# Graph attention and a top-2 mixture of experts on one Trainium2 core: negated scores, routing moved four steps behind its group, and gates applied by GpSimd as it scatters

## What is computed

```python
x = x + gnn(layernorm(x), adj)       # x: 2048 x 128, adj: 2048 x 2048 of 0 and 1
x = x + ffn(layernorm(x))            # 64 experts, top 2 of them for each row

def gnn(n, adj):
    h = n @ W.T + b_W
    e = (h @ a1)[:, None] + (h @ a2)[None, :] + b_a
    e = where(e > 0, e, 0.2 * e)
    return softmax(where(adj > 0, e, -9e15), axis=1) @ h

def ffn(n):
    top, idx = top_k(n @ Wr + br, 2)
    gates = softmax(top)                                 # two gates for each row
    combine[row, idx] = gates                            # 2048 x 64
    return sum over e of combine[:, e] * (relu(n @ W1[e] + b1[e]) @ W2[e] + b2[e])
```

## Time and profile before

| | |
|---|---|
| median of 3 runs | 335.87 us (334.42 to 335.96) |
| the profiled execution | 333.78 us, span 332.0 us |
| busy over the span | PE 223.2 us, DVE 216.4, ACT 143.9, POOL 185.0 |
| attention loop on DVE, to the last leaky | 24.8 to 139.7 us |
| last attend ends, first gather starts | 151.3 and 178.4 us |
| experts at speed | 224 to 312.8 us |
| end stage | 312.8 to 332 us |

### The profile page before, as it was taken

The page is one execution under the profiler, slowest core; times in us unless marked ns, Lnnn a source line. Parts: engine busy times, 40 slices in busy tenths (PEclk is TensorE's granted clock), DMA queues, the critical chain, the costliest instruction groups (busy, mean ns, idle before and its releaser), DMA issues.

```text
span 332.0 us, 6227 instructions
## 1 busy us (share of the span) xinstructions
PE 223.2 (67%) x1797; PEld 212.2 (64%) x1797; DVE 216.4 (65%) x583; ACT 143.9 (43%) x313; POOL 185.0 (56%) x210
## 2 busy tenths in 40 slices
PE   0790888999589579793431510209999999999830
PEld 0760788989589478793320410209999989999830
DVE  3859999999999299756734000005666756676476
ACT  1146858888862477632500200015664333444400
POOL 5510068998779867887774777773234323333300
PEclk9997899999989859998555585558999999999995
DMA  6993505998976200010111632213555656664184
GB/s 162 158 183 66 102 0 94 287 248 217 238 197 190 105 17 2 24 34 25 48 48 37 180 88 64 56 40 105 162 155 160 179 147 172 170 178 136 34 243 137
DMA packets 29056, 40.55 MB, mean 122 GB/s; under 512 B 3744, under 2 KB 24416, under 8 KB 28000
## 3 DMA queue, kind: packets, MB, share of 16 engines
q1 hardware_dynamic: 23280, 25.14, 25.7%
q0 software_dynamic: 5376, 14.72, 20.0%
q10 hardware_dynamic: 368, 0.30, 0.5%
HBM read 43.27 MB, written 5.26 MB: 146 GB/s over the span
## 4 chain that ended last, share of the span: by engine, by line
PE 35%; DVE 20%; issue 18%; POOL 14%; DMA 4%; ACT 4%; another core or an unknown queue 4%; SPq 1%; DVEq 0%; POOLq 0%; ACTq 0%
PE bank L907 13%; PE bank L917 13%; POOL table L361 7%; DVE arena L570 6%; DVE xs L753 2%; POOL ve L341 2%; POOL rstd L343 2%; PE bank L785 2%; DMA xs<-in_x 2%; DMA arena<-result 1%; POOL rk L369 1%; PE bank L897 1%; PE bank L822 1%; PE bank L775 1%
## 5 line engine op out<-in xcount | busy, mean ns | idle before, releaser
L907 PE MATMUL bank<-arena 128*128 x380 | 61.4, 287 | 30.3 <-issue 19.8
L907 PEld LDWEIGHTS bank<-arena 128*128 128x128 f32 x380 | 52.2, 200 | 31.7 <-issue 31.5
L407 POOL DMA_INDIRECT result<-arena x32 | 30.8, 963 | 60.8 <-DVE arena L731 55.9
L487 ACT ACTIVATE arena<-bank,arena 128x128 f32<-128x128 f32 x95 | 34.9, 368 | 60.9 <-PE bank L907 31.5
L822 PE MATMUL bank<-arena 128*128 128x130 f32 x512 | 61.3, 278 | 0.0
L822 PEld LDWEIGHTS bank<-arena 128*128 128x128 f32 x512 | 59.9, 194 | 0.0
L917 PE MATMUL bank<-w2s,arena 128*128 x380 | 59.1, 279 | 1.0 <-issue 1.0
L731 DVE SCALAR_TENSOR_TENSOR arena<-bank,arena 128x128 f32 x95 | 33.3, 351 | 39.6 <-PE bank L917 21.8
L812 PE MATMUL bank<-ident,arena 128*128 128x128 f32 x256 | 36.0, 301 | 25.9 <-DVE arena L570 25.4
L724 DVE TENSOR_SCALAR arena<-bank,arena 128x128 f32<-128x128 f32 x95 | 33.1, 348 | 30.2 <-issue 16.1
L917 PEld LDWEIGHTS bank<-w2s,arena 128*128 128x128 f32 x380 | 51.0, 195 | 1.6 <-issue 1.6
(11 more groups left out here) (156 smaller groups left out, 268.8 us busy)
## 6 DMA issues: line engine op xcount, KB each, us to landing
...
table<-rows_out,pos POOLq DMA_INDIRECT x32
arena<-table,arena POOLq DMA_INDIRECT x32
```

What stands on the lines that cost most here:

```text
L487: act.activation(hT[:, p % UH, 0, :], hp(p, 0), ACT.Relu, bias=w1s[:, p % UW, HID:HID + 1]).then_inc(e_ha, 1)
L907: ins = pe.matmul(hp(p, b), w1s[:, p % UW, P * b:P * b + P], xT_all[:, bass.ds(column, P)], start=True, stop=True)
```

## The change

There are three parts.

*Negated scores.* ACT writes the row of scores negated, the penalty is positive, and z holds negated scores with their minimum, tneg. The constant of the upper branch is then tneg itself, so ACT's operations for v2 and c_hi go, and leaky subtracts and takes the smaller. The exponential gets scale -1.

*Routing.* Groups are 4, 4, 4, 2 and 2 tiles. `route_a` and `route_b` on PE are now in step z+1, `route_a` between turn and attend; `route_c` in z+2; `top2` and the counts in z+3; `place` on DVE in z+4, and POOL's scatters from z+4 on, one tile (two DMAs) for each step. ACT's norm stands ahead of evac. All loops are two to four steps shorter.

*Gates.* A row carries its gate in one more column (GATE_COL), and POOL multiplies a finished block by it before it scatters the block. POOL's `combine` goes; DVE makes comb in 32 operations, once, ahead of the experts, with one matrix for each of the two choices, and b2 is loaded twice to match. At the end eight additions of 128x512 replace the 32 products, and ACT issues half of the eight loads. PE's first `up` comes ahead of the third block's transpose.

```diff
@@ -20 +20 @@
-    START = [0, 4, 8, 11, 14, T]
+    START = [0, 4, 8, 12, 14, T]
@@ -23 +23 @@
-    SLOT = [0, GRP, 0, 3, 6]
+    SLOT = [0, GRP, 0, GRP, 6]
@@ -27,2 +27,2 @@
-    ROW = D + 1
-    ID_COL = D
+    ROW = D + 2
+    ID_COL, GATE_COL = D, D + 1
...
@@ -39,2 +39,2 @@
-    PENALTY = -(2.0 ** 53)
-    LOWEST = -3.0e38
+    PENALTY = 2.0 ** 53
+    HIGHEST = 3.0e38
...
@@ -295,2 +292 @@
-                for k in range(TOPK):
-                    sp.dma_start(zl[:, k, 4 * c:4 * c + 4, :], zt[:, k, 4 * c:4 * c + 4, :]).then_inc(d_z[c], 16)
+                sp.dma_start(zl[:, 0, 4 * c:4 * c + 4, :], zt[:, 0, 4 * c:4 * c + 4, :]).then_inc(d_z[c], 16)
@@ -364,10 +359,0 @@
-            def combine(q):
-                n = SIZE[q]
-                if q >= 1:
-                    pool.wait_ge(s_comb, q)
-                for k in range(TOPK):
-                    ins = pool.tensor_tensor(cm[:, k, 0:n, :], hot[:, k, kept(q), :],
-                                             gate[:, k, START[q]:START[q + 1]].rearrange("p (g e) -> p g e", e=1).to_broadcast([P, n, E]), ALU.mult)
-                link(ins)
-                pool.tensor_tensor(comb[:, START[q]:START[q + 1], :], cm[:, 0, 0:n, :], cm[:, 1, 0:n, :], ALU.add).then_inc(s_comb, 1)
@@ -378 +364 @@
-            for s in range(T + 7):
+            for s in range(T + 5):
@@ -385 +371 @@
-                    if s == z + 5 and q < COUNTED:
+                    if s == z + 3 and q < COUNTED:
@@ -387 +372,0 @@
@@ -389 +374 @@
-                        if s == z + 6 + (0 if z > T - 3 else (j + q // 2) // 2):
+                        if s == z + 4 + (j, j, max(0, j - 1), 0, 0)[q]:
@@ -391,2 +375,0 @@
-                    if q < 2 and s == z + 6:
-                        combine(q)
@@ -400,2 +382,0 @@
-            for q in range(2, NG):
-                combine(q)
@@ -406,0 +388,2 @@
+                pool.tensor_scalar(y_all[:, b, :], y_all[:, b, :], rows_in[:, b, GATE_COL:GATE_COL + 1], None, ALU.mult).then_inc(e_gated, 1)
+                pool.wait_ge(e_gated, b + 1)
@@ -415 +398,2 @@
-            act.dma_start(b2_s[:, :], b2).then_inc(d_small, 16)
+            for k in range(TOPK):
+                act.dma_start(b2_s[k * E:(k + 1) * E, :], b2).then_inc(d_small, 16)
@@ -422 +406 @@
-                act.activation(trow[:, 512 * b:512 * b + 512], bank[b][:, :], ACT.Copy).then_inc(s_trs, 1)
+                act.activation(trow[:, 512 * b:512 * b + 512], bank[b][:, :], ACT.Copy, scale=-1.0).then_inc(s_trs, 1)
@@ -430,4 +414,3 @@
-                act.activation(r8[:, t:t + 1], tmax[:, t:t + 1], ACT.Relu, bias=s8[:, t:t + 1], scale=1.0 - SLOPE).then_inc(s_rv, 1)
-                act.activation(v2[:, t:t + 1], tmax[:, t:t + 1], ACT.Copy, scale=-SLOPE).then_inc(s_rv, 1)
-                act.wait_ge(s_rv, 2 * (t + 1))
-                act.activation(c_lo[:, t:t + 1], r8[:, t:t + 1], ACT.Identity, bias=v2[:, t:t + 1], scale=-1.0).then_inc(s_lo, 1)
+                act.activation(r8[:, t:t + 1], tneg[:, t:t + 1], ACT.Relu, bias=s8[:, t:t + 1], scale=SLOPE - 1.0).then_inc(s_rv, 1)
+                act.wait_ge(s_rv, t + 1)
+                act.activation(c_lo[:, t:t + 1], tneg[:, t:t + 1], ACT.Identity, bias=r8[:, t:t + 1], scale=-SLOPE).then_inc(s_lo, 1)
@@ -436 +418,0 @@
-                act.activation(c_hi[:, t:t + 1], c_lo[:, t:t + 1], ACT.Identity, bias=s8[:, t:t + 1]).then_inc(s_hi, 1)
@@ -445 +427 @@
-                                   bank[b][:, :], ACT.Exp).then_inc(s_ea, 1)
+                                   bank[b][:, :], ACT.Exp, scale=-1.0).then_inc(s_ea, 1)
@@ -464 +446 @@
-            for s in range(T + 7):
+            for s in range(T + 4):
@@ -467,2 +448,0 @@
-                if 1 <= s <= T:
-                    evac(s - 1)
@@ -470,0 +451,2 @@
+                if 1 <= s <= T:
+                    evac(s - 1)
@@ -472 +454 @@
-                    if s == START[q + 1] + 3:
+                    if s == START[q + 1] + 2:
@@ -474 +456 @@
-                    if s == START[q + 1] + 5:
+                    if s == START[q + 1] + 3:
@@ -499 +481,6 @@
-                act.activation(combT[:, START[q] * P:START[q + 1] * P], bank[q][0:E, 0:SIZE[q] * P], ACT.Copy).then_inc(s_cts, 1)
+                act.activation(combT[:, START[q] * P:START[q + 1] * P], bank[q][:, 0:SIZE[q] * P], ACT.Copy).then_inc(s_cts, 1)
+            act.wait_ge(e_put, 16 * NB)
+            zt = result.rearrange("(k t p) d -> p k t d", k=TOPK, p=P)
+            for c in range(4):
+                act.dma_start(zl[:, 1, 4 * c:4 * c + 4, :], zt[:, 1, 4 * c:4 * c + 4, :]).then_inc(d_z[c], 16)
...
@@ -564 +551 @@
-                                         scalar=LOWEST, op0=ALU.add, op1=ALU.max, accum_out=tmax[:, t:t + 1]).then_inc(s_z, 1)
+                                         scalar=HIGHEST, op0=ALU.add, op1=ALU.min, accum_out=tneg[:, t:t + 1]).then_inc(s_z, 1)
@@ -568 +554,0 @@
-                dve.wait_ge(s_hi, t + 1)
@@ -570 +556 @@
-                dve.scalar_tensor_tensor(z, z, c_hi[:, t:t + 1], low(t), ALU.add, ALU.max).then_inc(s_lk, 1)
+                dve.scalar_tensor_tensor(z, z, tneg[:, t:t + 1], low(t), ALU.subtract, ALU.min).then_inc(s_lk, 1)
...
@@ -598 +585 @@
-                    dve.wait_ge(s_comb, min(q - 1, 2))
+                    dve.wait_ge(s_cnt, min(q - 1, 2))
...
@@ -616,2 +602,0 @@
-                if 1 <= q <= 2:
-                    dve.wait_ge(s_comb, q)
@@ -623 +608 @@
-                link(dve.scalar_tensor_tensor(posf[:, :, 0:n], idxf[:, 0:n, :].rearrange("p g k -> p k g"), float(N),
+                link(dve.scalar_tensor_tensor(posf[:, :, 0:n], idxf[:, rows, :].rearrange("p g k -> p k g"), float(N),
@@ -626,0 +612 @@
+                dve.tensor_copy(rows_out[:, rows, :, GATE_COL], gate[:, :, rows].rearrange("p k g -> p g k"))
@@ -650 +636 @@
-            for s in range(1, T + 7):
+            for s in range(1, T + 5):
@@ -662 +648 @@
-                    if s == START[q + 1] + 6:
+                    if s == START[q + 1] + 4:
@@ -718,0 +705,4 @@
+            for t in range(T):
+                for k in range(TOPK):
+                    ins = dve.tensor_scalar(comb[:, t, k, :], iota_e, idxf[:, t, k:k + 1], gate[:, k, t:t + 1], ALU.is_equal, ALU.mult)
+            ins.then_inc(s_comb, 1)
@@ -752,3 +742,2 @@
-                    for t in range(4 * c, 4 * c + 4):
-                        ins = dve.scalar_tensor_tensor(xs[:, t, :], zl[:, k, t, :], gate[:, k, t:t + 1], xs[:, t, :], ALU.mult, ALU.add)
-                    ins.then_inc(done, 1)
+                    ct = slice(4 * c, 4 * c + 4)
+                    dve.tensor_tensor(xs[:, ct, :], zl[:, k, ct, :], xs[:, ct, :], ALU.add).then_inc(done, 1)
@@ -858 +847 @@
-            for s in range(T + 7):
+            for s in range(T + 3):
@@ -860,0 +850,3 @@
+                for q in range(NG):
+                    if s == START[q + 1] + 1:
+                        route_a(q)
@@ -864,3 +856 @@
-                    if s == START[q + 1] + 2:
-                        route_a(q)
-                    if s == START[q + 1] + 3:
+                    if s == START[q + 1] + 1:
@@ -868,2 +858 @@
-                for q in range(NG):
-                    if s == START[q + 1] + 4:
+                    if s == START[q + 1] + 2:
@@ -927,2 +916,2 @@
-            for b in range(3):
-                take(b)
+            take(0)
+            take(1)
@@ -929,0 +919 @@
+            take(2)
@@ -943 +933 @@
-                pe.wait_ge(s_comb, q + 1)
+                pe.wait_ge(s_comb, 1)
@@ -945 +935 @@
-                    ins = pe.transpose(bank[q][0:E, P * g:P * g + P], comb[:, START[q] + g, :], ident[:, :])
+                    ins = pe.transpose(bank[q][:, P * g:P * g + P], comb[:, START[q] + g, :, :].rearrange("p k e -> p (k e)"), ident[:, :])
```

32 lines of the change are left out of this document (15 added, 17 removed).

## The result

| | before | after |
|---|---|---|
| median | 335.89 us (4 runs) | 342.27 us (341.13 to 343.54, 4 runs) |
| profiled span | 332.0 us | 339.4 us |
| last leaky ends | 139.7 us | 156.7 us |
| last attend ends | 151.3 us | 168.1 us |
| first gather starts | 178.4 us | 185.9 us |

The account below looks back on a forecast made before the run. DVE was taken to pace the attention loop and PE the expert products. Start +0.3, loop +9.8, tail -3.6, gather to experts 0 and end -2.1 gave +4.4 us: 340.3 us forecast, range 328 to 348.

Parts of the forecast that it names:

- The likeliest case: Whole kernel: waits in the loop form as forecast and the gather-to-experts stretch is unchanged; 340.3 us, 337 to 344, chance 0.38.
- Wait A: Loop, ACT's norm ahead of evac: low comes late and DVE idles before leaky, 6.45 us over four tiles.
- Wait B: Loop, group's transposes ahead of attend on PE: DVE's residual waits at tiles 4, 8, 12; 8.5 us in all.
- The loop: Up to the end of the last attend: +9.8 us, to about 161 us; a further +0.3 is for the start.
- the close race of nm for tile 7: Loop: twice an nm starts within 0.2 us of a leaky's start; both taken as won, each loss 2.1 us more.
- What fell away: Loop: all waits before leaky go, -7.7 us, and POOL's combines, which stretched one z and one penalty, -0.8 us.
- The tail: Last attend to first gather, 27.1 us before: residual(15) and last nm come earlier; -3.6 us.
- not bound: Tail: the last four scatters follow pos by 5 us, the gather index came some 12 us behind pos.
- Gather to experts: First gather until PE is at speed: stalled stretch unchanged, covering DVE's comb; 0 us, bounds -4 and +3.
- The rival of a moving stretch: PE's releases before 224 us, some 10 us apart: one more or fewer gives 350 or 330 us; chance 0.1.
- The end: Gates on POOL, eight additions for DVE's 32 products: 2.7 us saved, 0.6 for the last bare multiply; sum -2.1 us.
- the second rival: Loop: POOL becomes the bound, two or three lost races at 2.1 us each; 344 to 347 us, chance 0.2.

Follow-up runs that it names:

- after_again: The changed kernel, unchanged, run and profiled a second time: ratio 1.0208 to the kernel before.
- norm_behind_evac: The changed kernel with ACT evacuating a tile's banks before it writes the row of the tile two back, as before the change: ratio 1.0308 to the kernel before.
- scatters_behind: The changed kernel with all 32 scatters moved behind the loop on POOL: 370.5 us, ratio 1.105 to the kernel before.
- parts_1_and_3: The changed kernel with the loop of the kernel before, keeping negated scores and gates on POOL: ratio 0.9815 to the kernel before (329.5 us).
- the second pair: Second profiles of the unchanged kernels before and after: last attend ends at 154.5 and 169.4 us, first gather at 180.0 and 187.4.
- the first set: One of four sets of runs, each with its own kernel before; here that took 304.65 us, in the three others 335.7, 335.2 and 335.1.
- both_orders_back: The changed kernel with evacuation ahead of the row on ACT and the group's transposes behind attend on PE: ratio 0.9920 to the kernel before.

## Why the prediction was right

The likeliest case came true, at 342.3 us for 340.3: waits A and B formed where they were forecast and made the loop longer. That the number came within 2 us is luck. The loop was 6.7 us above its term and the tail 5.7 below its own, and these cancelled; the loop alone would have put the time at 347, outside the forecast's own 337 to 344 and at the edge of the range.

- **Wait A**: forecast 6.45 us at tiles 4, 6, 10 and 14. Measured 5.7 in four waits: 2.10, 1.42, 0.17 and 2.05, at tiles 4, 6, 10 and 14. The step-by-step walk from the earlier trace rows holds.
- **Wait B**: forecast 2.6, 2.9 and 3.0 us, 8.5 in all. Measured 2.44, 8.53 and 2.73, 13.7 (in after_again 4.08, 8.69 and 2.73, 15.5). The mechanism was right, and two sizes in the first trace. The term for group 1 was mis-sized by 5.6 us, for two reasons that I left to the range or left out. I had taken the close race of nm for tile 7 as won, and it was lost. And I priced the attend behind waiting transposes at its 3.75 us of the earlier trace rows, where after 6 us of an idle PE it took 5.78. In the sliced page the granted clock falls to 0.7 and 0.8 there; and in norm_behind_evac, with the longest waits, the 512 attend products had a mean of 298 ns against 278 before. The length of PE's wait alone does not set the price, though. Group 0's rows in after_again:

```profile
69.89 0.66 PE L819 MATMUL bank<-ident,rows_out 128*128 128x128 f32 x4 [2.38 <-ACT rows_out L432]
70.38 5.40 PE L811 MATMUL bank<-arena 128*128 128x130 f32 x32
```

The wait is 2.38 us and the attend takes 5.40, with a granted clock of 0.68 in its window; group 1 of scatters_behind has the same wait of 2.38 us, and the attend behind it takes 3.75 at 1.00. Nor had I looked at attends outside the three groups: rinv waits 2.7 us at tiles 0, 2 and 7, of which the kernel before had 0.6. These terms (+5.2, +2.2, -0.7) make the 6.7 us by which the loop passed its +10.1.
- **What fell away**: I counted all of the 7.7 us before leaky and 0.8 of combines as gone. parts_1_and_3 shows 4.4 us left with the old loop. In the changed loop the waits' places are others, so the term can't be read there alone; but forecast for parts 1 and 3 it would have given -10.3 us by this sum (-7.7, -0.8, -2.1, +0.3), and they gave 6.2.
- **The tail**: forecast -3.6 us, measured -9.3 (-7.5 by the second pair). From the last attend to the counts' total on PE it is 8.3 us for 12.7, -4.4, near the forecast. The other 4.9 lie in the chain of small operations behind it. The kernel before, then the kernel after:

```profile
172.63 0.61 PE L887 MATMUL bank<-arena,ones_f 64*128 64x32 f32 x2
```

```profile
177.55 0.19 DVE L694 SCALAR_TENSOR_TENSOR arena<-iota_p,bank 128x32 f32<-128x32 f32 x1 [3.10 <-PE bank L889]
```

```profile
183.68 0.61 PE L876 MATMUL bank<-arena,ones_f 64*128 64x32 f32 x2
```

```profile
185.04 0.19 DVE L680 SCALAR_TENSOR_TENSOR arena<-iota_p,bank 128x32 f32<-128x32 f32 x1 [0.34 <-PE bank L876]
```

From the end of the same product to the same operation it is 4.3 us before and 0.75 after. POOL scatters back to back until 175.1 in the one and until 183.3 in the other. This looks like the late news of the gathers, and the other traces bear it out: in the four of the first set these 4.3 us are 0.04, in the other ten 0.75 to 6.9. So the part of the tail that came as a gift is one that changes from trace to trace. The forecast also called the scatters "not bound". In the traces of the first set the first gather waits for them: it starts 2.12 us after the last scatter, when that has landed. In the kernel after the last scatter ends at 183.27, and with the same 2.12 us the gather could have started at 185.39 at the earliest; it started at 185.86. So this tail could have been only 0.5 us shorter before the scatters bound it.
- **Gather to experts**: forecast 0, measured +0.1; the stretch moved with the gathers, and comb stayed hidden in it (DVE rests there in the kernel after too). Without the long stretch it is not quite hidden: in both_orders_back DVE's first relu starts at 187.09, behind comb, for a product that ended at 186.11. The rival of a moving stretch did not come in these two traces, but it was the right thing to doubt: between sets it is worth 31 us, two to three times the 10 to 14 us that the rival gave it.
- **The end**: forecast -2.1 us, measured -1.4. The bare multiply is 0.6 us (L388, 606 ns), as taken. The two additions behind the last landing are 1.42 for 1.35. The eight loads keep the DMA engines at 0.98 for 10.0 us (325.2 to 335.2). Before it was 9.4 us at 0.86 (0.97 from 317.0 on), with some 0.2 MB less moved in it: the stores of the output began 3.1 us before its end, and 4.3 us in the kernel after. The engines are full with one issuer and with two: the splitting brought nothing that shows. The Trainium skill, page DMA: Bandwidth & Descriptors, section "Issuing engines are not separate DMA queues", says that several issuers save only issue time, and the trace agrees. The experts' stage was forecast unchanged and is 1.2 us longer; its products' granted clock reads 0.97 for 0.98, and I have no run on it.
- **The rivals**: waits A and B did form. POOL lost one race of the two or three by which the second rival would reach 344 to 347 us.
